# Splitting queries and keys in the accumulator, folding biases, and one product of the mixing on GpSimd: a transformer layer on one core

## What is computed

```python
# x: (16, 512, 256), all float32
q, k, v = split(x @ qkv_w + qkv_b)                # 16 heads of 16
local  = window_attention(q, k, v)                # a query's last 128 keys (dist > 0 and <= 128)
pooled = mean of x over chunks of 8 tokens        # 64 latents
rq = x @ rq_w + rq_b ; rk, rv = split(pooled @ rkv_w + rkv_b)
remote = softmax(rq rk^T / 4, chunks before) rv @ rout_w + rout_b
gate   = sigmoid(local @ gl_w + remote @ gr_w)    # one number for a token and head
mixed  = gate * local + (1 - gate) * remote
x1 = layernorm(x + mixed @ out_w + out_b)
h  = gelu(rms_norm(x1) @ ternary(w_up).T)
y  = layernorm(x1 + rms_norm(h) @ ternary(w_down).T)
```

## Time and profile before

| what | value |
|---|---|
| median of 3 runs | 1172.92 us (1170.47 to 1173.93) |
| the profiled execution | 1173.3 us |
| its span | 1171.6 us |
| TensorE busy | 982.2 us (84%) |
| VectorE busy | 933.7 us (80%) |
| ScalarE busy | 686.3 us (59%) |
| GpSimd busy | 703.8 us (60%) |
| mean granted clock of TensorE | 0.926 of full |

### The profile page before, as it was taken

How to read it: one execution, slowest core, us unless ns; L and a number is a source line. 1 busy time by engine, 2 the same in 40 slices (tenths; PEclk the granted TensorE clock), 3 DMA queues, 4 the chain that set the end, 5 groups by cost and what they waited for, 6 DMA issues and landing times. The chain is left out here.

```text
span 1171.6 us, 36746 instructions
## 1 busy us (share of the span) xinstructions
PE 982.2 (84%) x15202; PEld 634.5 (54%) x15202; DVE 933.7 (80%) x1928; ACT 686.3 (59%) x1093; POOL 703.8 (60%) x881
## 2 busy tenths in 40 slices
PE   5768898989988898998889898888988888884855
PEld 3445564656556565555646555565656555562523
DVE  6479879797988978798897979889897978875554
ACT  3424665657576565757656575756656576662544
POOL 7205765565667566566756656675665667673664
PEclk8879999999999999999999999999999999996787
DMA  7730604325070522507043340705234150601000
GB/s 220 204 103 27 172 30 120 100 66 154 5 215 4 153 67 75 144 4 216 3 136 83 86 134 4 216 4 163 57 101 119 48 153 4 187 16 37 1 20 18
DMA packets 58179, 107.50 MB, mean 92 GB/s; under 512 B 19718, under 2 KB 38038, under 8 KB 54934
## 3 DMA queue, kind: packets, MB, share of 16 engines
q1 hardware_dynamic: 57868, 105.15, 32.1%
q10 hardware_dynamic: 144, 0.00, 0.0%
HBM read 70.93 MB, written 33.55 MB: 89 GB/s over the span
## 5 line engine op out<-in xcount | busy, mean ns | idle before, releaser
L824 ACT ACTIVATE Pt<-scores 128x1024 f32<-128x1024 f32 (+1 forms) x256 | 230.0, 917 | 147.7 <-PE oacc L1508 83.7
L1091 DVE TENSOR_REDUCE nmax<-work 128x3 f32<-128x480 f32 x352 | 215.6, 634 | 37.0 <-PE work L1462 33.7
L677 POOL TENSOR_TENSOR h_lo<-hbuf,h_hi 128x512 f16<-128x512 f32 x128 | 148.0, 1156 | 157.4 <-DVE h_hi L1222 157.4
L649 POOL TENSOR_SCALAR_AFFINE_SELECT Pt<-Pt 128x512 f32<-128x512 f32 x256 | 164.1, 641 | 99.8 <-ACT Pt L824 99.2
L1508 PE MATMUL oacc<-Pt,Vp 128*32 128x256 f32 (+1 forms) x2048 | 155.7, 362 | 15.2 <-POOL Pt L653 8.5
L1457 PE MATMUL work<-Ks,Qs 98*32 98x160 bf16 x4096 | 150.4, 240 | 16.1 <-DVE nmax L1091 11.7
L636 POOL TENSOR_TENSOR parts<-Pt,parts 128x512 bf16<-128x512 f32 x64 | 72.9, 1158 | 136.0 <-ACT parts L749 136.0
L1488 PE MATMUL scores<-Qs,Ks 100*32 100x160 bf16 (+4 forms) x4096 | 126.9, 239 | 29.7 <-ACT Pt L824 14.1
L1521 PE MATMUL oacc<-wdn_t,h_hi 128*128 128x256 f16 x512 | 125.5, 283 | 18.0 <-POOL h_lo L677 18.0
L1488 PEld LDWEIGHTS scores<-Qs,Ks 100*32 100x32 bf16 x4096 | 87.8, 102 | 77.8 <-ACT Pt L824 47.6
L1521 PE MATMUL oacc<-wdn_t,h_lo 128*128 128x256 f16 x512 | 125.4, 283 | 0.0
(11 more groups left out here) (159 smaller groups left out, 1910.2 us busy)
## 6 DMA issues: line engine op xcount, KB each, us to landing
parts_scratch<-parts SPq DMA_DIRECT2D x96, 256.0 KB, 5.3
Qs<-parts_scratch SPq DMA_DIRECT2D x96, 256.0 KB, 5.1
Ks<-parts_scratch SPq DMA_DIRECT2D x96, 256.0 KB, 4.8
xT<-x_t SPq DMA_DIRECT2D x16, 512.0 KB, 6.7
xres<-x SPq DMA_DIRECT2D x16, 512.0 KB, 7.7
y<-nat SPq DMA_DIRECT2D x16, 512.0 KB, 3.1
Qs<-nmax_pair SPq DMA_DIRECT2D x256, 2.0 KB, 1.7
nat<-up_t SPq DMA_DIRECT2D x1, 1024.0 KB, 7.7
```

The costliest lines, as they stand in the source:

```text
L649: ins = pool.affine_select(out=pt[:, :, 0:P], in_=pt[:, :, 0:P], compare_op=ALU.is_gt, fill=0.0, base=0, pattern=[[0, 4], [1, P]], channel ...
L677: pool.tensor_tensor(h_lo[:, t % NR, :], hbuf[:, t % 2, :], h_hi[:, t % NR, :], ALU.subtract).then_inc(h_lo_ready, 1)
L824: nc.scalar.activation(Pt[:, u % NPT, :, 0:w], scores[:, slot, :, :].rearrange("p k (h q) -> p (k h) q", h=2)[:, :, 0:w], ACT.Exp, scale=S ...
L1091: nc.vector.tensor_reduce(nmax[:, first:first + n], work[:, slot, 0:n * BAND].rearrange("p (h c) -> p h c", h=n), X, ALU.max, negate=True) ...
```

## The change

It has five parts.

1. *Queries and keys.* After ScalarE's copy of a part, TensorE adds minus that part to the same PSUM bank: a matmul of the bf16 part with minus the identity (`minusb`). ScalarE then copies the bank again, with the bias each time, as the next part. `qk_rest`, VectorE's subtraction and GpSimd's are gone. Eight new steps `SPLIT` to `SPLIT + 7` stand in the lists; a bank is released by ScalarE after part 2.
2. *The remainder of xn.* In the same way: TensorE adds minus `xnT[0]` to the transposed xn, ScalarE copies the rest (`XN_LO`).
3. *Biases.* The bias of the values no longer goes into `Vp`: ScalarE copies the values plain. It is folded into the gate's bias, into the output bias (`bv` through `out_w`) and, negative, into the remote part's bias, and put into the first row by `dead`. The bias of the remote part is added in SBUF by GpSimd (`bias_remote`, two instructions), and VectorE transposes the remote part out of PSUM.
4. *Mixing.* GpSimd multiplies `rem` by `ng`, in two halves, and then makes the four additions of the output bias to the residual. VectorE makes both products with o and then adds and transposes one half after the other.
5. *Maxima.* `split_maxima` moves to behind the second tile of the feed-forward part, and `move_max` behind `restack` (not in the last two sequences).

Setup: nine more loads on SP's queue in front of the weights' semaphore, and a few small operations.

```diff
 SECOND_HALF = (
-    ("F", GATE), ("P", QK), ("P", QK + 1), ("P", QK + 2), ("F", OUT), ("P", QK + 3),
-    ("F", OUT + 1), ("P", LAT_RQ), ("P", LAT_RKV), ("P", VALUES), ("P", LAT_SCORES), ("F", NORM),
+    ("F", GATE), ("P", QK), ("P", QK + 1), ("P", SPLIT), ("P", QK + 2), ("P", SPLIT + 1), ("P", SPLIT + 2),
+    ("F", OUT), ("P", QK + 3), ("P", SPLIT + 3), ("P", SPLIT + 4), ("F", OUT + 1), ("P", SPLIT + 5), ("P", SPLIT + 6),
+    ("P", LAT_RQ), ("P", SPLIT + 7), ("P", LAT_RKV), ("P", VALUES), ("P", LAT_SCORES), ("F", NORM),
     ("F", NORM + 1), ("P", LAT_EXP), ("P", VALUES + 1), ("F", XN_T), ("F", XN_T + 1), ("F", XN_HI),
     ("P", LAT_EXP + 1), ("F", XN_LO), ("P", VALUES + 2), ("F", UP), ("P", LAT_NORM), ("F", UP + 1),
...
+SPLIT_AT = ("F", UP + 1)
...
 # SyncE, body
-                if not s.last:
+                if s.i == B - 2:
                     move_max(s.next())
                 if not s.first:
                     store_before(s)
                 if later.exists:
                     restack(later)
+                    move_max(s.next())
...
 # GpSimd
-                    pool.tensor_tensor(parts[:, 2, t, :], qk_rest[:, t, :], parts[:, 1, t, :],
-                                       ALU.subtract).then_inc(part2, 1)
...
+                if k == GATE:
+                    pool.wait_ge(rem_biased, count(s, 1, 0))
+                    for i in range(2):
+                        if i == 0:
+                            pool.wait_ge(gate_ng, count(s, 1, 0))
...
+                        pool.tensor_tensor(of_half, of_half, ng.unsqueeze(3).to_broadcast([P, KT, G32, HD]),
+                                           ALU.mult).then_inc(mix_part, 1)
+                    for b in range(NB):
+                        add_bias(s, b)
...
+            def bias_remote(s):
...
+                for t in range(KT):
+                    ins = pool.tensor_tensor(rem[:, s.par, t, :, :], rem[:, s.par, t, :, :],
+                                             rem_b[:, t, :].unsqueeze(1).to_broadcast([P, G32, 2 * HD]), ALU.add)
+                ins.then_inc(rem_biased, 1)
...
 # GpSimd, body: behind the masks
-                for b in range(NB):
-                    add_bias(s, b)
+                if s.next().exists and not s.first:
+                    bias_remote(s.next())
...
 # ScalarE
-                        nc.scalar.activation(parts[:, 1, t, :], qk_rest[:, t, :], ACT.Copy).then_inc(part1, 1)
+                if SPLIT <= k < SPLIT + 8:
+                    t, j = (k - SPLIT) // 2, (k - SPLIT) % 2 + 1
...
+                    act.wait_ge((rest1, rest2)[j - 1], count(s, 4, t))
+                    nc.scalar.activation(parts[:, j, t, :], p_bank(bank), ACT.Identity, bias=bqk[:, t:t + 1]
+                                         ).then_inc((part1, part2)[j - 1], 1)
...
+                if VALUES <= k < VALUES + NB:
...
+                    nc.scalar.activation(of_heads[:, :, 0:VN],
+                                         p_bank(bank)[:, 0:H * VN].rearrange("p (h d) -> p h d", d=VN), ACT.Copy
+                                         ).then_inc(p_taken[bank], 1)
...
-                            ins = nc.scalar.activation(remT[:, t, i * HALF:(i + 1) * HALF],
...
+                if k == XN_LO:
+                    for t in range(KT):
+                        act.wait_ge(xn_rest, count(s, KT, t))
+                        nc.scalar.activation(xnT[:, 1, t, :], oacc[:, t, :], ACT.Copy).then_inc(xn_lo, 1)
...
 # VectorE
-                    nc.vector.scalar_tensor_tensor(out=qk_rest[:, t, :], in0=p_bank(bank),
...
-                        nc.vector.tensor_tensor(xnT[:, 1, t, :], oacc[:, t, :], xnT[:, 0, t, :], ALU.subtract
-                                                ).then_inc(xn_lo, 1)
...
-                        mark(nc.vector.tensor_tensor(
-                            half_rem, half_rem, of_half(gate[:, 2, :, :, :], i).rearrange(
-                                "p t b m -> p t (b m)").unsqueeze(3).to_broadcast([P, KT, G32, HD]), ALU.mult))
-                        sync()
+                    sync()
+                    for i in range(2):
+                        dve.wait_ge(mix_part, count(s, 2, i))
                         done(nc.vector.tensor_tensor(mixed[:, i, :, :], mixed[:, i, :, :],
...
 # TensorE
+                if SPLIT <= k < SPLIT + 8:
+                    t, j = (k - SPLIT) // 2, (k - SPLIT) % 2
...
+                    pe.wait_ge((part0, part1)[j], count(s, 4, t))
+                    nc.tensor.matmul(p_bank(bank), minusb[:, :], parts[:, j, t, :], start=False, stop=(j == 1),
+                                     skip_group_check=True).then_inc((rest1, rest2)[j], 1)
...
+                if k == XN_LO:
+                    for t in range(KT):
+                        pe.wait_ge(xn_hi, count(s, KT, t))
+                        nc.tensor.matmul(oacc[:, t, :], minus[:, :], xnT[:, 0, t, :], start=False, stop=True,
+                                         skip_group_check=True).then_inc(xn_rest, 1)
```

More of the change, by code:

```diff
@@ L136, in order_of_prologue @@
     order += [("P", 0, LAT_T), ("P", 0, LAT_T + 1)]
-    order += [("P", 1, QK + c) for c in range(4)]
+    order += [("P", 1, k) for k in split]
     order += [("P", 0, LAT_O), ("P", 1, LAT_RQ), ("P", 1, LAT_RKV), ("W", 0, SUMS)]
@@ L453, in build @@
         ]
+        for c in range(4):
+            for q_tile, v in ((bv_q, v_b), (rem_b, rout_b)):
+                loads.append((q_tile[c * GT:(c + 1) * GT, :, :],
+                              bass.AP(v.tensor, v.offset + c * 2 * HD, [[0, GT], [P, KT], [1, 2 * HD]])))
         ff_loads, wqk_load, loads = loads[:2], loads[2], loads[3:]
@@ L719, in body @@
                         f_step(s, k)
-                    elif later.exists:
-                        p_step(later, k)
             for phase, i, k in PROLOGUE:
@@ L819, in weights @@
                     act.wait_ge(pv_done, count(s, NU, u - NPT))
-                if u == 1 and not s.last:
-                    act.wait_ge(part2, count(s.next(), 4, 3))
                 w = 2 * P if u % NB < NB - 1 else P
@@ L1281, in body @@
                         ternary_down((2, 5, 8).index(u))
-                    if u == A_STEPS and not s.last:
-                        split_maxima(s.next())
+                if s.i == B - 2:
+                    split_maxima(s.next())
                 later = s.second_next()
@@ L1503, in weigh @@
                     pe.wait_ge(o_taken, count(s, HG, hg - 2))
+                if s.first and v == 0:
+                    pe.wait_ge(bias_ready, 1)
+                    pe.wait_ge(gate_bias, 2)
                 pe.wait_ge(masked, count(s, NU, v))
```

201 lines of the change are left out of this document (106 added, 95 removed).

## The result

The changed kernel takes 1217.22 us (median of 4 runs, 1209.46 to 1217.8), the kernel before on the same chip 1171.7 us (4 runs, 1167.72 to 1173.93). The ratio is 1.0377, 95% interval 1.0326 to 1.0428: slower by 45.5 us, 6 us over the forecast of 1211 and inside its range.

What follows compares the result with a forecast made beforehand. A chain through VectorE, TensorE and ScalarE bounds each sequence, ScalarE running alone at its end. 14 x (3.1 - 0.7) = 33.6, plus 0.3, 2.7 and 2, makes 38.6 us: forecast 1211, range 1195 to 1232.

Steps and rivals of the forecast that it cites:

- The main term: Mixing: two-input operations of VectorE and GpSimd alternate strictly, each waiting for the other's end; `mixT` comes 2.4 us later.
- the o products did not take 0.69 beside GpSimd's: Rival in the mixing: no collision between VectorE and GpSimd, `mixT` at 591.5, total 1177 us; chance 0.13.
- `xn` came later and not 2.5 us earlier: Rival before `xn`: VectorE sets the pace, its relief reaches `nbias`, a sequence gains 1.45 us, total 1156; chance 0.12.
- GpSimd's product took 1.26 (mean) and not 2.3: Rival in the mixing: GpSimd's products cost twice 1.16 us, `mixT` another 2.3 us later, total 1247; chance 0.1.
- the transfers of the maxima had landed in time: Rival on SP's queue: `nmax` transfers land over 3.4 us later than counted; 5 us would give 1232; chance 0.05.
- From `mixT` to `xn`: Output product to first `xn`: five splits on TensorE, VectorE's value take and stall gone; `xn` 1.3 us later.
- ScalarE's copies: First `xn` to first GELU: two value copies and two `xnT` remainder copies add 1.75 us unhidden; GELU 3.1 later.
- The GELU stage: Both TensorE idle stretches (0.63, 0.69) close, the maxima's split costs 0.5 to 0.6 us; net 0.7 earlier.
- The prologue: Start: nine more loads before the weights' semaphore, less work taken off ScalarE's and GpSimd's queues: an estimated 2 us.
- The ends: Last two sequences: sequence 14 costs 0.3 us for the remainder path, sequence 15 costs 2.7 for `mixT` with nothing beside it.

Runs made afterwards that it cites:

- the kernel with early additions: Changed kernel with the residual additions back behind the masks and the remote bias moved behind x1, GpSimd still making both products: 1191.3 us (ratio 1.0195).

## Why the prediction came out as it did

**The main term was right, in mechanism and nearly in size.** VectorE and GpSimd alternate, each to the other's end. `mixT` was to be 2.4 us later and is 2.58: from `ng` on it took what I counted (2.16 more, 2.2 forecast), and the gate in front of it lost 0.42 behind `bias_remote` (L1180 starts 2.89 us after the gate's first operation, L1154 2.47) where I had counted 0.2. That part 4 is the cause is shown from both sides: put alone on the kernel before it costs 27 us, and taking it and `bias_remote` out of the changed kernel gives 50. The forecast's 1.02 us for a GpSimd product that has waited has no row behind it; from the end of the o product to its own end the second took 0.92. No rival holds: the o products did not take 0.69 beside GpSimd's, `xn` came later and not 2.5 us earlier, GpSimd's product took 1.26 (mean) and not 2.3, and the transfers of the maxima had landed in time (the view of waits has two waits of TensorE for them, 12.9 us in all; before, two with 12.5).

The Trainium skill ("GPSIMD Engine Reference", 1. Specifications) names a VectorE instruction with two SBUF inputs, or one in a 2-port mode, as what contends with GpSimd for SBUF. The runs agree for two inputs: the o product waits to the end of GpSimd's two-input product. The entry says nothing of GpSimd's own inputs; with one there the o product lost 0.4 us. Whether `h_hi`, which waits with one input, runs in a 2-port mode, no run here shows. Of the ratio of about two ("GPSIMD Engine Reference", 4.1 Engine selection) the runs show 1.5 for the first product, which did not wait (1.06 us against 0.69), and 1.8 for the mean (1.26). The same entry calls one-input work on GpSimd roughly line-rate; beside VectorE it took 1.48 to 2.05 us here, more than the two-input product.

**From `mixT` to `xn`: too short by 0.7 us in the short form, blind to the long one.** I forecast `xn` 1.3 us later; it is 2.0 later in the short form and 3.7 in the long. The 0.7 lie all along the way: `mixT` 0.2, the way from the output product to the latent keys and from there to `lat_bd` some 0.4 (8.17 us and 2.6 for the forecast 7.9 and 2.4), and the rest behind `lat_bd`. And I counted no change of clock, and eight of thirteen sequences lost 1.7 us to it: 13.6 us, the largest thing that I missed. The same wait was followed by full clock in the other five. In the kernel before, the 2.27 us before `lat_bd` were followed by full clock in the sequence of the earlier trace rows and in no other of the first fourteen. So a stretch of 2.2 us puts the clock at risk here and does not decide it, and the one sequence that I read hid this risk.

**ScalarE's copies: right in mechanism, the basis not typical.** 1.75 us forecast in front of the first GELU; from the first `xn` it took 6.94 us, forecast 7.15, with no gap. But the forecast's 5.40 was that of the one sequence at full clock. Against the median of 5.73 the copies added 1.2 us, because the change also gave TensorE its clock back in this stretch. That is 0.55 less than forecast and nearly hides the 0.7 of the step in front: the first GELU of the short form is 3.2 later, forecast 3.1. That these two agree is luck. Undoing the remainder's pair gave 15.2 us and undoing the two value copies in that stretch 6.1.

**The GELU stage: 0.56 instead of 0.7, mechanism right in part.** TensorE's wait for `h_lo` (0.63) is gone, but that for `h_sum` did not close: it is 0.58, where it was 0.69. The split of the maxima, priced at 0.5 to 0.6, costs 0.37 by the run that moved it back.

**Not foreseen, in the change's favour.** From the row sums to the next gate a sequence takes 24.7 us instead of 25.6 (means of 0 to 13). The windows view of the kernel before shows where 0.6 of it lay:

```profile
627.48:630.96 3.48, 3.48 (x32) 2.41 (x32) 1.17 (x4) 0.00 (x0) 1.61 (x2) 0.64 0.00 0
```

These 3.48 us lie between the row sums and the first scores, and the granted clock is 0.64. In nine of the fourteen sequences before the stretch takes 3.1 to 3.5 us at 0.64 to 0.75, in the other five 2.37 at 1.00; the mean is 3.01. After the change it takes 2.37 us at 1.00 in all. TensorE had stood 0.63 and 0.69 us just ahead of it, but so it had in most of the five at full clock; that the shorter waits keep the clock up fits the rows and was not tested alone. 0.9 times 14 is 13 us, and it is luck that this and the long forms nearly cancel: without the long forms the forecast would have been some 7 us too high, without this 19 too low.

**The prologue: term mis-sized, and its reason wrong.** I gave 2 us to nine more loads; it was 4.35. The kernel without part 1 has the same nine loads and the same folding of biases and reaches its first gate at 111.30, against 111.41 before. So they cost nothing there. The ten kernels with part 1 reach it at 115.8 to 118.8. TensorE's timeline in the changed kernel shows the chain of part 1:

```profile
18.25 0.60 PE L1381 MATMUL scores<-parts,minusb 128*128 128x512 bf16 x2 [1.55 <-ACT parts L782]
20.23 0.61 PE L1381 MATMUL scores<-parts,minusb 128*128 128x512 bf16 x1 [1.37 <-ACT parts L782]
...
32.26 5.62 PE L1353 MATMUL scores<-wv,xT 128*128 128x272 f32 x16 [2.75 <-DVE wrog L985]
```

With little beside it, TensorE and ScalarE pass each bank to and fro and each waits for the other. The wait for `wrog` isn't part 1's. The values product in the kernel without part 1, and in the kernel before:

```profile
29.39 6.29 PE L1381 MATMUL scores<-wv,xT 128*128 128x272 f32 x16 [5.92 <-DVE wrog L985]
```

```profile
26.16 6.36 PE L1332 MATMUL scores<-wv,xT 128*128 128x272 f32 x16 [1.50 <-DVE wrog L939]
```

It starts at 29.39 and 26.16 there, at 32.26 here. The folding thus delays that product by 3.2 us, which does not reach the first scores (84.56 without part 1, 84.65 before); part 1 delays it by 2.9 more, and the first scores come at 88.02.

**The ends.** The last sequence cost 2.14 (forecast 2.7), sequence 14 gave 0.16 (forecast +0.3).

In all: 38.6 us forecast, 44.0 measured between the profiled executions: +2.35 prologue, -0.55 and -0.45 at the ends, and +4.1 in the fourteen sequences, in which 13.6 of clock are lost, 13 given back behind the row sums, and 3.4 come from the first GELU of the short form (3.2 later, forecast 3.1, the sum of the two misses above) and the GELU stage.

## What to carry to other kernels

A relief of the busiest engine was worth nothing here, because its work went to an engine that it then had to wait for: look for VectorE operations with both inputs in SBUF, and for conversions to float16 there, that will run beside two-input operations of GpSimd, and count them to the end of GpSimd's. Before a stage is read from one sequence, look at the granted clock of the same stage in the others. An operation that moves should go to a place where its new engine waits and nothing of the chain stands behind it; a copy of the values taken off ScalarE brought the first GELU forward by 0.35 us in one place and put `xn` back by 0.5 in another. Undo a mixed change part by part: here parts 1 and 3, the latter with `bias_remote` and two copies moved, held a gain of 2.5% behind three parts that cost more.

## What the runs showed of the hardware that was not expected

- What waits for a two-input GpSimd operation isn't told by the number of VectorE's inputs alone. Over all traces here `h_hi`, one input and a conversion to float16 in SBUF, takes 0.43 us alone and ends 0.28 (both medians) behind GpSimd's operation when it meets one (1.09 in the row above). A transposition of 512 elements in SBUF keeps its 0.71 beside the residual additions, and the residual's sum with `work`, one input of which comes from PSUM, its 0.68 to 0.69 beside GpSimd's subtraction.
- A GpSimd operation with one input delays a two-input VectorE operation by 0.4 us (1.10 against 0.69) and is itself slow beside it (1.48 to 2.05 us for 512 elements).
- Even a VectorE operation on 2 elements a partition takes 1.10 instead of 0.15 us when it meets a two-input GpSimd operation: the delay goes by GpSimd's duration, not by its own.
- After 2.2 us without work the next stretch of TensorE's work, 3.7 us at full clock, took 5.4 in eight of thirteen sequences; after 1.80 us, in the kernel with early additions, in none. Eight dummy matmuls in the stretch removed it, which was worth 15 us by the medians and 10 by the ratios.
- In the kernel before, a wait of 2.27 us before the latent scores went with a granted clock of 0.78 to 0.80 up to the first GELU in thirteen of fourteen sequences; after the change, with a wait of 0.87 us, it was full in all.
